# The last stage of a four-stage kernel: two streams set apart in time, and the second round's opening placed beside the first round

## The reference

```python
n1 = _layernorm(x, ln1_w, ln1_b)
rw = _gating(n1, smha_sim, smha_gates, 2)             # normalised logits, top 2, masked softmax over 8
q = einsum('btc,ech,bte->bth', n1, q_proj, rw)        # k and v alike: 8 experts of 128x128
attn = softmax(causal(q @ k.T / sqrt(128))) @ v
hs = x + einsum('bth,ehc,bte->btc', attn, o_proj, rw)
n2 = _layernorm(hs, ln2_w, ln2_b)
rw2 = _gating(n2, moe_sim, moe_gates, 2)
out = hs + einsum('btei,eic,bte->btc', gelu(einsum('btc,eci->btei', n2, w1)), w2, rw2)
```

## Time and profile before

| | us |
|---|---|
| median of three runs | 3150.83 |
| the profiled execution's own time | 3154.66 |
| its span | 3152.5 |
| PE, DVE, ACT, POOL busy (whole span) | 2425.7, 2198.9, 1710.0, 1415.3 |
| granted TensorE clock (whole span) | 0.869 of full |

### The profile page before, as it was taken

How to read it: one execution, slowest core, us unless ns; L and a number is a source line. 1 busy time by engine, 2 the same in 40 slices (tenths; PEclk the granted TensorE clock), 3 DMA queues, 4 the chain that set the end, 5 groups by cost and what they waited for, 6 DMA issues and landing times.

```text
span 3152.5 us, 42236 instructions
## 1 busy us (share of the span) xinstructions
PE 2425.7 (77%) x15570; PEld 1750.1 (56%) x15570; DVE 2198.9 (70%) x3701; ACT 1710.0 (54%) x2608; POOL 1415.3 (45%) x1331
## 2 busy tenths in 40 slices
PE   3114776677667687799999999999999569876987
PEld 1002455344345565477777777777777456755675
DVE  3995698699699612588878887887888543355334
ACT  4223664666376242588777877787778323222332
POOL 0341144144224300365765676657656641564156
PEclk8556888788788888799999999999999879887988
DMA  3000000000000000100000010010000100000000
GB/s 100 0 0 0 0 1 1 1 1 1 1 1 1 1 1 14 41 21 21 21 21 21 21 28 21 20 26 21 21 24 9 41 1 1 1 14 1 1 1 14
DMA packets 32029, 42.02 MB, mean 13 GB/s; under 512 B 8897, under 2 KB 18130, under 8 KB 31442
## 3 DMA queue, kind: packets, MB, share of 16 engines
q1 hardware_dynamic: 31826, 39.34, 4.6%
HBM read 12.05 MB, written 2.10 MB: 4 GB/s over the span
## 4 chain that ended last, share of the span: by engine, by line
PE 46%; issue 19%; DVE 17%; POOL 12%; ACT 4%; SPq 1%; DMA 0%; POOLq 0%; ACTq 0%; DVEq 0%
PE ps L954 10%; PE ps L932 6%; PE ps L943 6%; POOL MA L379 5%; DVE MA L1090 3%; PE ps L710 3%; PE ps L914 2%; PE ps L1723 2%; DVE lnb L265 2%; PE ps L645 2%; PE ps L647 1%; PE ps L646 1%; PE ps L1665 1%; POOL MA L1173 1%; PE ps L1625 1%
## 5 line engine op out<-in xcount | busy, mean ns | idle before, releaser
L1090 DVE TENSOR_REDUCE MA<-ps 128x1 f32<-128x1024 f32 x512 | 623.3, 1221 | 195.3 <-PE ps L932 182.7
L379 POOL TENSOR_TENSOR MA<-MA,BIG 128x1024 f32<-128x1024 f32 x120 | 280.2, 2356 | 624.9 <-DVE BIG L350 624.9
L954 PE MATMUL ps<-MA,WB 128*64 128x128 f32 x4096 | 502.5, 276 | 0.0
L954 PEld LDWEIGHTS ps<-MA,WB 128*64 128x64 f32 x4096 | 440.7, 137 | 88.4 <-issue 87.4
L344 DVE TENSOR_TENSOR_SCAN BIG<-BIG 128x1024 f32<-128x1024 f32 x128 | 347.1, 2751 | 0.0
L932 PE MATMUL ps<-BIG 96*128 96x512 f16 x1024 | 314.6, 389 | 13.5 <-ACT WB L1017 5.1
L632 ACT ACTIVATE HR<-ps,b 128x512 f32<-128x512 f32 x288 | 191.6, 687 | 243.9 <-PE ps L647 242.9
L710 PEld LDWEIGHTS ps<-WB,HR 128*128 128x128 f32 x2304 | 307.3, 210 | 24.9 <-issue 8.6
L710 PE MATMUL ps<-WB,HR 128*128 128x128 f32 x2304 | 314.4, 295 | 0.0
L1017 ACT ACTIVATE WB<-ps,MA 128x1024 f32<-128x1024 f32 x206 | 229.6, 1115 | 149.8 <-DVE MA L1090 149.8
L497 PE MATMUL ps<-bc,sel 96*128 96x512 bf16 x256 | 108.3, 520 | 247.1 <-DVE BIG L350 190.8
(11 more groups left out here) (290 smaller groups left out, 5166.3 us busy)
## 6 DMA issues: line engine op xcount, KB each, us to landing
BIG<-BIG SPq DMA_DIRECT2D x192, 64.0 KB, 2.0
BIG<-WB SPq DMA_DIRECT2D x192, 64.0 KB, 2.0
WB<-w_dram SPq DMA_DIRECT2D x1, 2304.0 KB, 14.7
X<-x_dram SPq DMA_DIRECT2D x4, 512.0 KB, 12.6
HR<-w_dram SPq DMA_DIRECT2D x1, 2048.0 KB, 9.4
out_dram<-X SPq DMA_DIRECT2D x4, 512.0 KB, 3.2
WB<-wqkv_dram SPq DMA_DIRECT2D x1, 1536.0 KB, 6.7
WB<-w_dram SPq DMA_DIRECT2D x2, 512.0 KB, 9.1
```

The costliest lines, as they stand in the source:

```text
L379: e.tensor_tensor(yy[:, c, :], yy[:, c, :], db[n % 2][c], ALU.add).then_inc(*p_my.up(b, n, c))
L954: x = e.matmul(bank[6][64 * pp:64 * pp + 64, 0:128], V[(4 * b + g) % 2][:, k, 64 * pp:64 * pp + 64], DT[n % 2][:, 128 * k:128 * k + 128], ...
L1090: e.tensor_reduce(L_of(n)[:, c:c + 1], ps[s][:, :], AX, ALU.max, negate=True).then_inc(*v_amx.up(n, s))
```

## The change

It rewrites the order of the last stage and some of its operations.

* The plan: D_PERIOD 159 for 193. The generators of stream 1 are all delayed by D_SHIFT = 20 (`later`). The openings of both rounds become generators of their own (`front_*`), the one of round 1 with due times from 27 to 120 of round 0, in single instructions 0.95 apart. The closes are generators too (`last_dve`, `last_pool`); that of round 0 is due from 186 on, 27 units into round 1.
* New buffers, so that the two rounds can overlap: `s_hs` and `s_n1` for each round (n1 of round 1 in the old `sel` tile), gate values of round 1 in the old `acc` tile, and `s_tmp` for the weighted expert results.
* The squares for the gate: eight ScalarE `Square` instructions with `accum_out` replace L1469 and L1330.
* The transposes and logits of round 1's opening use banks 2 and 3 of the stream ("the output projection's banks") between its attention and its output projection; step 17's transposes (in round 0) wait for the gate to have read the logits, and the two banks swap roles in that round.
* The close's add to x moves from GpSimd (L1502) to VectorE, in two halves.

```diff
-        D_PERIOD, D_EXPERT, D_SHIFT = 193.0, 3.15, 0.0
-        D_LN = [(0, 3), (5, 8), (139.5, 142.5), (187.5, 190.5)]
-        D_TR = [11, 110, 145.5]
-        D_GATE = [(13, 16, 19, 22), (145.5, 148.5, 151.5, 154.5)]
+        D_PERIOD, D_EXPERT, D_SHIFT = 159.0, 3.15, 20.0
+        F_AT, F_TURN, F_SQ, F_LOGITS = [(0, 0.25), (27, 0.95)], [12.8, 110.2], [(14.2, 0.25), (76.4, 0.95)], [14.4, 110.8]
+        F_GATE = [(16.5, 17.5, 18, 21), (85, 113.5, 116, 120)]
+        D_LN, D_CLOSE, D_TURN, D_SQ, D_LOGITS = (139.6, 0.25), [(186, 0.6), (186, 0.25)], 147.2, (148.9, 0.25), 148.8
+        D_GATE = (151.5, 152, 152.5, 155.5)
         D_ATT = [76.4 + 3.5 * i + 0.1 * i * (i - 1) for i in range(9)]
-        D_OUT, D_STEP, D_MOE, D_MSTEP = 111, 1.6, 157, 1.75
+        D_OUT, D_STEP, D_MOE, D_MSTEP = 111, 1.6, 152.2, 1.75
...
+        def d_ln(e, k, r, w, src, dst, at, ready, free=None):
+            s, (t, f) = st[f"d{k}"], at
+            for j in range(8):
+                yield t + f * j
...
+                i = e.bn_stats(s[:, j, 0:6], src[j])
...
+            yield t + f * 8
...
+            for j in range(8):
+                yield t + f * (14 + j)
+                if j == 0:
+                    e.wait_ge(*p_dln[k].at(r, w, "rstd"))
...
+                i = e.tensor_scalar(dst[:, j, :], src[j], s[:, j, 6:7], s[:, j, 9:10], ALU.subtract, ALU.mult)
...
+        def last_dve(e, k, r):
+            t, f = D_CLOSE[r]
+            yield from d_ln(e, k, r, 3, [s_hs[k][r][:, j, :] for j in range(8)], lnb[k], (d_at(r, t), f),
+                            {0: p_dm[k].at(r, 15)}, v_dx[k].at(r - 1) if r else None)
...
+        def front_pool(e, k, r):
+            t, f = F_AT[r]
+            for w in range(2):
+                yield t + f * (22 * w + 8.2)
+                d_root(e, k, r, w)
+            yield F_GATE[r][0]
+            d_norm(e, k, r, 0)
...
+        def d_squares(e, k, r, w, at):
+            g, (t, f) = s_g[k][r if w == 0 else 0], at
+            for j in range(8):
+                yield t + f * j
...
+                i = e.activation(s_sq[k][:, j, :], s_n1[k][r][:, j, :], ACT.Square, bias=0.0, scale=1.0,
+                                 accum_out=g[:, j, 56:57])
...
+        def front_pe(e, k, r):
+            B = bank[4 * k:4 * k + 4]
+            yield F_TURN[r]
+            d_turn(e, k, r, 0, B[2:4] if r else B)
+            yield F_LOGITS[r]
+            d_logits(e, k, r, 0, B[2])
...
                         elif q == 16:
-                            e.wait_ge(*a_dat[k].at(r, "turn", 7, 1))
+                            e.wait_ge(*(a_dat[k].at(r, "turn", 7, 1) if r else a_dtr[k].at(1, 0, 1)))
                         else:
-                            e.wait_ge(*v_dat[k].at(r, "out", 7))
+                            e.wait_ge(*(v_dat[k].at(r, "out", 7) if r else v_dgt[k].at(1, 0, "logits")))
...
-            weave(experts_dve(e), soft_dve(e, 0), soft_dve(e, 1))
+            weave(experts_dve(e),
+                  *[later(g, D_SHIFT * k) for k in range(2) for g in
+                    (front_dve(e, k, 0), front_dve(e, k, 1), soft_dve(e, k), last_dve(e, k, 0), last_dve(e, k, 1))])
```

More of the change, by code:

```diff
@@ L1206, in parts, with d_proj, two @@
+        def d_proj(r, q, more=0.0):
+            return d_at(r, 25 + 26.2 * (q // 8) + D_EXPERT * (q % 8) + more)
         def parts(i):
             return range((i + 4) // 4)
-        def two(name, *ordered):
-            return [Tick(sem(f"{name}{k}"), [(r, *x) for r in range(2) for x in ordered]) for k in range(2)]
-        t_dtr = two("t_dtr", (0, 0), (0, 1), (0, "logits"), (2, 0), (2, 1), (2, "logits"))
+        def two(name, *ordered, front=()):
+            order = [(0, *x) for x in front] + [(1, *x) for x in front] if front else []
+            order += [(r, *x) for r in range(2) for x in ordered]
+            return [Tick(sem(f"{name}{k}"), order) for k in range(2)]
@@ L1214, in program @@
+        t_dtr = two("t_dtr", (2, 0), (2, 1), (2, "logits"), front=((0, 0), (0, 1), (0, "logits")))
         t_dst = two("t_dst", *keys(32))
@@ L1304, in soft_dve, with front_dve @@
+        def front_dve(e, k, r):
+            hs, (t, f) = s_hs[k][r], F_AT[r]
+            yield from d_ln(e, k, r, 0, [tile_of(k + 2 * r, j) for j in range(8)], hs, (t, f), {})
+            yield from d_ln(e, k, r, 1, [hs[:, j, :] for j in range(8)], s_n1[k][r], (t + 22 * f, f),
+                            {0: v_dln[k].at(r, 0, "out")})
+            yield from d_gate(e, k, r, 0, F_GATE[r], bank[4 * k + 2])
         def soft_dve(e, k):
-            s, L = st[f"d{k}"], s_L[k]
-            hs, n1 = s_hs[k], s_n1[k]
@@ L1307, in soft_dve @@
-            hst, n1t = [hs[:, j, :] for j in range(8)], [n1[:, j, :] for j in range(8)]
-            B, S0, S1 = bank[4 * k:4 * k + 4], ps[2 * k], ps[2 * k + 1]
+            L = s_L[k]
+            B, S0 = bank[4 * k:4 * k + 4], ps[2 * k]
             def G(i):
[L1311 to L1324, removed]
@@ new lines, in d_turn, with d_logits @@
+        def d_turn(e, k, r, w, banks):
+            for h in range(2):
+                e.wait_ge(*v_dln[k].at(r, max(w, 1), "out"))
+                if w == 0 and r:
+                    e.wait_ge(*(v_dat[k].at(0, "out", 7) if h else a_dat[k].at(0, "turn", 7, 1)))
+                for j in range(4):
+                    i = e.transpose(banks[h][:, 128 * j:128 * j + 128], s_n1[k][r][:, 4 * h + j, :], ident[:, :])
+                i.then_inc(*t_dtr[k].up(r, w, h))
+        def d_logits(e, k, r, w, o):
+            e.wait_ge(*a_dtr[k].at(r, w, 1))
+            if w:
+                e.wait_ge(*v_dom[k].at(r, 1))
+            elif r == 0:
+                e.wait_ge(*v_dsp.at("simn"))
+            for j in range(8):
+                i = e.matmul(o[:, 8 * j:8 * j + 8], xT[k][:, 128 * j:128 * j + 128], simn[:, w // 2, :], start=True, stop=True)
+            i.then_inc(*t_dtr[k].up(r, w, "logits"))
@@ L1784, in _ @@
             e.wait_ge(phase, 8)
-            weave(experts_pe(e), soft_pe(e, 0), soft_pe(e, 1))
+            weave(experts_pe(e),
+                  *[later(g, D_SHIFT * k) for k in range(2) for g in (front_pe(e, k, 0), front_pe(e, k, 1), soft_pe(e, k))])
         @block.scalar
@@ L1794, in _ @@
             e.wait_ge(phase, 8)
-            weave(experts_act(e), soft_act(e, 0), soft_act(e, 1))
+            weave(experts_act(e),
+                  *[later(g, D_SHIFT * k) for k in range(2) for g in (front_act(e, k, 0), front_act(e, k, 1), middle_act(e, k), soft_act(e, k))])
         @block.vector
@@ L1814, in _ @@
             e.wait_ge(phase, 8)
[L1815 removed]
+            weave(experts_pool(e),
+                  *[later(g, D_SHIFT * k) for k in range(2) for g in
+                    (front_pool(e, k, 0), front_pool(e, k, 1), soft_pool(e, k), last_pool(e, k, 0), last_pool(e, k, 1))])
         @block.sync
```

425 lines of the change are left out of this document (212 added, 213 removed).

## The result

| | before | after |
|---|---|---|
| median of 20 runs, us | 3150.92 (3148.19 to 3154.84) | 3155.52 (3152.74 to 3164.52) |
| the profiled execution's own time | 3154.66 | 3153.58 |
| its span | 3152.5 | 3151.8 |
| start of the last stage (first `st_d` on VectorE) | 2505.4 | 2500.4 |
| length of the last stage | 647.1 | 651.4 |

The ratio of the times is 1.0016, with a 95% interval from 1.0009 to 1.0023. I had forecast 3087 with a range up to 3128. The three first stages ended 5 us earlier in the profiled execution of after than in that of before, so the two stages are compared by their lengths.

A forecast was written before the change was run, and what follows sets the result against it. TensorE's own work was taken as the last stage's floor, 461 us; 439 after the start gave 3024, waits of 51 gave 3075, the end's 15.2 a span of 3090. Forecast 3087, range 3048 to 3128.

The forecast's parts named there:

- rival 4: No change: the offset costs at both ends and in the start what the middles give; 3150 us, chance 0.03.
- The start: Last stage to about 2585: stream 1's opening holds up stream 0's queues; loses about 12 us against before.
- Step (a): Round 1's opening beside round 0: each of its four GpSimd roots delays the next scaling, 1.5 us each, 6 us.
- Work: TensorE's own work in the last stage at full clock: 230.6 us a round, 461 in all.
- Attention: Waits in attention: 5.5 us a round for copies within the transposes, 3 for others; 17 for two rounds.
- Rival 3: Slower: each attention piece waits for its own chain, the other stream's products queued behind; 95 us, 3182, chance 0.10.
- The middles: Layer norm between output projection and experts, partly uncovered by the other stream: 9 us for stream 0, 10 for stream 1.
- (b): Round 1's opening: its transposes and logits wait, with stream 1's attention products queued behind; 4.5 us per stream, 9.
- The end: From the last product, stream 1's alone, through the close to the store: 15.2 us, before 19.2.
- The squares: Gate squares on ScalarE: 8 pairs taken at 4.3 us, 2.9 without the accumulator read.
- Rival 2: ScalarE changes tables for the squares: 39 blocks, 36 more loads, 46 us of ScalarE; 3118 us, chance 0.20.
- Rival 1: Better cover: waits (a) to (e) mostly filled, 20 us instead of 51; 3056 us, chance 0.17.

The follow-up runs named there:

- late roots: Changed kernel (offset 20) with GpSimd's roots of openings and closes due at 14.5 spacings in place of 8.2: 3148.56 us; also tried at other offsets.
- the split: Changed kernel (offset 20) with the second part of an attention block's transposes on TensorE given its own due time, 0.6 later: 3148.98 us.
- the form with two inputs: Changed kernel (offset 20) with the layer norms' scaling (L1338) as scalar_tensor_tensor in place of tensor_scalar: 3155.45 us.

## Why the prediction was wrong

The sign was wrong: the forecast was 3087 with 0.87 on faster, the result is 0.16% above before, nearest in time to rival 4, which had 0.03. One sign that I had named did come: no stretch of 25 us after the start has TensorE under two thirds busy (the lowest is 17.2 of 25). It went with no gain, since the full stretches were lost. The clock, forecast at 1.00 throughout, is below it in 9 of the 22 such stretches, down to 0.73. Of the stage, 651.4 for 584.6, a miss of 66.8 us, is made up as follows.

**The start was right within 3 us.** I counted 22 us of work in the first 80 and the trace has 24.5. So were its steps. The first scaling ended at 2537.05, 36.7 us after the stage's start, against 39.2 forecast; the third at 2548.32, 47.9 against 50.9:

```profile
2534.08 0.25 POOL L248 TENSOR_SCALAR st_d<-st_d 128x8 f32<-128x8 f32 x1 [8.98 <-DVE st_d L1330]
...
2536.04 2.05 POOL L1518 TENSOR_TENSOR BIG<-MA,BIG 128x512 f32<-128x512 f32 x2
...
2545.35 0.25 POOL L248 TENSOR_SCALAR st_d<-st_d 128x8 f32<-128x8 f32 x1 [7.25 <-DVE st_d L1330]
...
2547.32 2.05 POOL L1518 TENSOR_TENSOR BIG<-MA,BIG 128x512 f32<-128x512 f32 x2
...
2548.42 1.12 PE L1671 MATMUL ps<-ident,BIG 128*128 128x128 f32 x4 [3.73 <-POOL BIG L1518]
...
2563.04 0.25 POOL L248 TENSOR_SCALAR st_d<-st_d 128x8 f32<-128x8 f32 x1 [12.38 <-DVE st_d L1330]
```

Stream 1's roots stand ahead of stream 0's scalings, as I had read from the due times. The third root (2563.04), the first of round 1's opening by its due time, held GpSimd for 12.38 us and wasn't in my list; that the sum came out right in spite of it is in part luck. What I failed to do was to carry this on: a root ahead of scalings comes back with every opening and close.

**Step (a) is the one that failed most: 6 us forecast, 32.6 measured** (after the first 80: L1671 for L1518 20.9, for L1428 7.3, L1767 for L1518 4.4). Of these, 7.1 went with the late roots and 11.3 lie at the boundary; the waits for VectorE's split (L1428) and in the output projection weren't taken apart. I priced a root by its own 2 us and took VectorE to be on time, because it was busy for 21 of 79 us. But the price of a root in GpSimd's queue is its length and the time that its input is late, up to 12.4 us in the rows above and 10.5 in those of offset 0. A mean busy share says nothing of that lateness. Moving the roots alone gave 7 us at offset 20, 15 at 10 and 23 at 0.

Not all of (a) are roots; at offset 20 the larger part isn't. The longest wait after the start lies in the boundary of the rounds, and I had let that boundary pass with "the close lies beside products". Its timeline in after:

```profile
2870.39 2.35 DVE L1484 TENSOR_TENSOR X<-X,lnb 128x512 f32<-128x512 f32 x2
...
2870.56 1.64 POOL L1531 TENSOR_TENSOR MA<-MA,BIG 128x512 f32<-128x512 f32 x1 [2.75 <-DVE BIG L1470]
2872.67 0.68 DVE L1470 TENSOR_TENSOR BIG<-ps,BIG 128x512 f32<-128x512 f32 x1
...
2873.43 1.26 POOL L1531 TENSOR_TENSOR MA<-MA,BIG 128x512 f32<-128x512 f32 x1 [1.23 <-DVE BIG L1470]
2874.64 3.06 POOL L1518 TENSOR_TENSOR BIG<-sel,acc 128x512 f32<-128x512 f32 x3
2877.75 1.12 PE L1671 MATMUL ps<-ident,BIG 128*128 128x128 f32 x4 [6.37 <-POOL BIG L1518]
```

Read it backwards: TensorE waits 6.37 us for scalings of round 1; on GpSimd they stand behind the adds of the other stream's experts (L1531); these wait for the weighting on VectorE (L1470), which stands behind the close's add to x (L1484), moved there by this change. But that add accounts for at most 1.6 us of the 6.37: the 1.23 us for which GpSimd waits, and some 0.34 by which the first L1531 is longer beside it (1.64, elsewhere 1.30). The rest is the order itself: two adds of experts, the first after another wait of 2.75 us for its weighting, ahead of a scaling for which TensorE has nothing else. No run took the add away, so this split is read from the rows only. Waits of TensorE for L1518 between 2829 and 2900 come to 14.8 us, and to 11.3 with late roots. I had priced that add only at the end of the kernel, where it saves 1 us.

**Clock: 19.7 us that I had left out.** I summed the rest at full clock, though the earlier trace rows have 0.50 to 0.66 around the holes. In the windows where the holes were the clock did come back (1.00 for 0.66 and for 0.53), but the stretches that were full have 0.94 to 0.97 where before there was 0.98 to 1.00. The 19.7 are still less than the 26.0 of before; what failed is that I took it as nothing. At offset 0 the late roots gained as much by the clock (11.5) as by idle time (11.3).

**Work: 10.4 us that I had taken as fixed.** It is 460.6 at offset 0 and 460.9 before, 464.6 at offset 5, 468.7 at 7, and 470 to 471 from 10 on. So it comes with the offset, not with the openings in pieces. It isn't slower products: where a product of another type (fp16 or fp32) follows at once, the one ahead of it takes no longer than others of its line (151 such places in after, 0.2 us in all). The extra lies in the last product ahead of each gap, whose record counts until its (modelled) end and not until the next product's start. Against the median of its line that is 5.8 us in 39 gaps before, 5.8 in 38 at offset 0, and 13.5 in 85 gaps in after: 7.7 of the 10.5 us, some 0.16 for each. So the same idle time in twice as many pieces costs more than the idle column shows.

**Attention: 17 forecast, 29.2 measured** (L1682 12.2, L1742 11.0, L1752 6.0). The 11 us for the second part of the transposes were right to the decimal (16 waits, up to 0.7). New are the 10.4 us of scores waiting for an exponential. I kept 3 a round for such things; ScalarE also has the squares and the other stream's projections there; which of them delays the exponential I did not take apart. Rival 3 had this mechanism with 2 us and more in each of 32 steps; it was 8 steps, of up to 2.0, so that rival was wrong in size.

**The middles: 19 forecast, 24.0 measured** (L1641 16.6, L1808 7.4 after the first 80). **(b): 9 forecast, 3.0 measured**; the waits of step 17 for the gate's logits came once (2.3). **The end: 15.2 forecast, 15.2 measured**, but the match is luck: from the last product to the statistics I had 2.2 us and it took 3.2, the scalings I had at 3.2 and they took 2.2.

These are start −2.5, work +10.4, cold +19.7, idle +38.5 (89.5 for 51), tail 0: 66.1 of the 66.8. The rest is rounding in my own sum.

**The squares** cost less than I took: a pair of `Square` and accumulator read every 0.29 us, 8 in 2.34 us, below my lower bound of 2.9:

```profile
2520.94 0.30 ACT L1560 ACTIVATE BIG<-MA 128x128 f32<-128x128 f32 x1
...
2521.14 0.19 ACT L1560 ACTIVATION_READ_ACCUMULATOR BIG<-MA 128x1 f32 x1
```

Rival 2 fell: the stage has 11 table loads (12 forecast, 39 for the rival), none of them at a `Square`. 16 of the 64 ran with the Gelu's table loaded, and there is none either where a `Square` stands among copies just ahead of a Gelu:

```profile
2774.31 0.19 ACT L1560 ACTIVATION_READ_ACCUMULATOR BIG<-MA 128x1 f32 x1
2774.65 0.60 ACT L1627 ACTIVATE BIG<-ps 128x512 f32<-128x512 f32 x1 [0.16 <-PE ps L1767]
2775.27 1.28 ACT L1633 ACT_TABLE_LOAD   x1
2776.56 0.60 ACT L1633 ACTIVATE HR<-ps 128x512 f32<-128x512 f32 x1
```

**So where did the gain go?** It was there: the waits for the weights fell from 82.2 to 36.0, and the stretch 2819 to 2875 went from 15.3 to 44.6 busy. Against before the stage saved 5.4 us of idle time after the first 80, 6.3 at half clock and 4.0 at the end, and gave back 9.4 in the start, where the second stream comes late, and 10.5 in work, by the many gaps; sum +4.2. The holes that were closed came back as short waits, those in GpSimd's queue above all. Late roots and an offset of 7 (with the split) give 3106.4, 49 us less. Of the 44 us between the stages of after and of the kernel with offset 10 and late roots, the terms are: start 8.6, work 1, cold 10.0, idle 29.6, and the tail takes 5.2 back. Rival 1, 3056 by better cover, stayed out of reach in all of them: even at offset 7 there are 47.9 us idle and 20.9 cold.

**Open.** Why 14 is worse than a line between 10 and 20 is only located, not explained. Whether the slowed scalings on VectorE cost any time was not measured by itself, and it is a rival for part of the waits: they shrink from offset 20 to 10, as the time does, though offset 0 has hardly any and is no faster than 10. That the share of the closes in the 7 to 23 us of the late roots is small is likely, since TensorE has other products there, but openings and closes were moved together.

## What to carry to other kernels

Where each engine's order is fixed ahead, an instruction that waits for another engine costs the lateness of its input besides its length, and whatever stands behind it pays; give it the due time at which its result is needed, not that at which its input is planned to be there. Price a reordering by following each queue through all its repetitions, not only through the first. Make an offset between two streams about as long as the serial piece that it is to cover (here 5 to 10 units of about 1.5 us for 11 us did equally well, 20 cost 35 us more than 10 with late roots), and time the plan's parameters before judging the idea. Count the gaps too, not only their sum.

## What the runs showed of the hardware

VectorE's scalings of 128x128 with a scalar per row take about 340 ns alone. One that starts while GpSimd is in a tensor-tensor takes up to 1086 ns beside a scaling (L1518, 1047 ns) and up to 1294 beside an add (L1531, 1298 ns); eight of them took 5.81 us for 2.14. All 30 slowed ones of the stage end 81 to 87 ns after the GpSimd instruction that was running, so they wait for its end. The statistics, among the same instructions, stay at 279 (276 before). The Trainium skill, "SBUF — State Buffer", section "Who interferes with whom", says that VectorE and GpSimd share a pair of ports, that `tensor_scalar` can enter a mode that takes it, that an instruction with two SBUF inputs contends for it with GpSimd's reads, and that the other engine "**fully blocks**" for the whole instruction. The trace agrees, and the form with two inputs was slowed alike. The page adds that whoever issues first decides. The trace agrees here too: three of GpSimd's L1518 that started with some 0.22 us of a VectorE scaling still to run took 1132 or 1133 ns in place of 1047, as in

```profile
2759.66 1.13 POOL L1518 TENSOR_TENSOR BIG<-MA,BIG 128x512 f32<-128x512 f32 x1
```

so GpSimd is held up as well, but only by the rest of a short instruction; two with less than 0.15 us to run beside them took the usual 1047.

At a change of ScalarE's tables the next activation, where it has nothing else to wait for, starts where the load's 1.28 us end (2775.27 and 2776.56 above); no further drain is to be seen.
